# Attention scores and running maxima as pairs of 64-row matmuls, eight pairs to a group, in a one-core decoder layer

## What is computed

```python
q, k, v = (proj(Wq), proj(Wk), proj(Wv))             # H, DK = 16, 64
scores = jnp.einsum('bhqd,bhkd->bhqk', q, k)         # S = 2048
scores = scores + rel_bias[buckets(S)].transpose(2, 0, 1)[None]
attn = jax.nn.softmax(scores, axis=-1)
ctx = jnp.einsum('bhqk,bhkd->bhqd', attn, v)
```

## Time and profile before

| | |
|---|---|
| time, median of 3 runs | 3967.45 us (3962.96 to 3972.64) |
| span of the profiled execution | 3970.6 us |
| PE busy | 3864.0 us, 97% |
| DVE / ACT / POOL busy | 2459.6 / 2034.9 / 2685.8 us |
| granted clock of PE, mean | 0.989 |
| DMA, mean | 89 GB/s |

### The profile page before, as it was taken

One profiled execution on the slowest core, in us unless ns is written; L12 is line 12 of the kernel. 1 busy time (PEld: TensorE's weight loads), 2 busy tenths in 40 slices (PEclk: granted clock), 3 DMA queues, 4 the chain that ended last, 5 costly groups with the idle time before them and its releaser, 6 DMA issues. The chain is left out here.

```text
span 3970.6 us, 59813 instructions
## 1 busy us (share of the span) xinstructions
PE 3864.0 (97%) x18973; PEld 2189.4 (55%) x18973; DVE 2459.6 (62%) x3356; ACT 2034.9 (51%) x3452; POOL 2685.8 (68%) x1402
## 2 busy tenths in 40 slices
PE   8999999999999999999999999999997999997899
PEld 7754444444444444444444444444446888885477
DVE  3456666666666666666666666666634777775632
ACT  3335555555555555555555555555543555553232
POOL 1128888888888888888888888888893434430010
PEclk9989999999999999999999999999998999998999
DMA  7642222322222352222332222332312333335710
GB/s 222 168 104 57 62 60 62 94 74 62 62 59 62 93 161 60 64 60 59 87 85 60 64 59 60 88 83 59 100 34 83 107 101 103 106 104 174 278 45 22
DMA packets 395504, 352.29 MB, mean 89 GB/s; under 512 B 193947, under 2 KB 268187, under 8 KB 394008
## 3 DMA queue, kind: packets, MB, share of 16 engines
q1 hardware_dynamic: 326200, 321.84, 28.2%
q10 hardware_dynamic: 67168, 20.98, 2.2%
q0 software_dynamic: 1920, 6.29, 0.5%
HBM read 142.64 MB, written 89.70 MB: 59 GB/s over the span
## 5 line engine op out<-in xcount | busy, mean ns | idle before, releaser
L328 POOL TENSOR_TENSOR acc<-acc,probs 128x1024 f32<-128x1024 f32 x894 | 2127.2, 2379 | 263.5 <-ACT probs L798 138.7
L928 DVE TENSOR_REDUCE maxes<-ps 128x1 f32<-128x1024 f32 x1024 | 1251.2, 1222 | 700.9 <-PE ps L579 696.4
L801 ACT ACTIVATE probs<-ps,far_bias 128x1024 f32<-128x1024 f32 (+7 forms) x1280 | 1022.0, 820 | 1018.5 <-DVE near_s L945 561.2
L614 PE MATMUL ps<-probs,v_head 128*64 128x512 f32 x4096 | 992.2, 605 | 2.1 <-ACT ctx_out L784 2.0
L579 PE MATMUL ps<-stacks 64*128 64x512 f32 x2048 | 751.1, 447 | 16.4 <-issue 7.4
L594 PE MATMUL ps<-stacks 64*128 64x512 f32 x1792 | 662.1, 449 | 0.0
L593 PE MATMUL ps<-stacks 128*128 128x512 f32 x2048 | 619.2, 419 | 0.3 <-ACT probs L798 0.3
L594 PEld LDWEIGHTS ps<-stacks 64*128 64x128 f32 x1792 | 276.9, 185 | 501.0 <-issue 328.4
L614 PEld LDWEIGHTS ps<-probs,v_head 128*64 128x64 f32 x4096 | 248.6, 136 | 483.6 <-issue 481.4
L593 PEld LDWEIGHTS ps<-stacks 128*128 128x128 f32 x2048 | 351.3, 189 | 216.4 <-issue 164.0
L945 DVE TENSOR_TENSOR near_s<-ps,near_bias 128x384 f32<-128x384 f32 (+2 forms) x576 | 284.7, 494 | 268.9 <-PE ps L594 246.1
(11 more groups left out here) (281 smaller groups left out, 4751.7 us busy)
## 6 DMA issues: line engine op xcount, KB each, us to landing
stacks<-c_k SPq DMA_DIRECT2D x128, 256.0 KB, 2.5
stacks<-c_q SPq DMA_DIRECT2D x128, 256.0 KB, 2.6
stacks<-c_d SPq DMA_DIRECT2D x256, 128.0 KB, 2.7
scr_v<-probs ACTq DMA_DIRECT2D x32, 512.0 KB, 4.0
stacks<-c_q SPq DMA_DIRECT2D x128, 128.0 KB, 2.7
v_head<-scr_v SPq DMA_DIRECT2D x32, 512.0 KB, 3.6
scr_ctx<-ctx_out SPq DMA_DIRECT2D x128, 128.0 KB, 2.3
both_ctx<-scr_ctx SPq DMA_DIRECT2D x32, 512.0 KB, 4.0
```

The lines of the kernel that those rows point to most:

```text
L328: pool.tensor_tensor(acc[:, qb, :], acc[:, qb, :], pr, ALU.add).then_inc(s["summed"], 1)
L614: mm = pe.matmul(ps[64 * half:64 * half + 64, PV, :], v_head[:, side, kt, :], probs[:, st % PT_RING, half * 512:(half + 1) * 512], start=k ...
L801: ins = act.activation(probs[:, st % PT_RING, a:z], sc[:, a:z], ACT.Exp, bias=bias)
L928: dve.tensor_reduce(maxes[:, qt, pair:pair + 1], ps[:, bank:bank + 2, :], AX.XY, ALU.max).then_inc(s["max_done"], 1)
```

## The change

All score and maximum matmuls become 64-row matmuls in pairs that share the array: lanes 0 and 1 (rows 0 to 63 and 64 to 127) hold the same keys, and each owns half of the queries. A step is three pairs (key difference high by query high, by query low, and key difference low by query high), plus a guard pair in the first two steps of a queries half. A pair of maxima gives 512 keys against two tiles of queries. In a group PE does one pair of maxima, six pairs of scores, one pair of maxima in one run, then the projection, then the values. `stacks` is laid out anew, so `fill` issues 32 DMAs of 64 rows instead of 21; the guard row is loaded by two DMAs instead of one. On ACT and DVE both steps of a group come before the work of the projection that stood between them.

```diff
-FILLS_MAX, FILLS_SCORE = 16 * 2 * BLOCKS, 16 * (3 * BLOCKS + 1)
+FILLS_MAX, FILLS_SCORE, FILLS_GUARD = 16 * 3 * BLOCKS, 16 * 5 * BLOCKS, 32
...
 guard():
-                sp.dma_start(stacks[0:1, side, QB, half * QW:(half + 1) * QW]...).then_inc(s["neg_in"], 16)
+                for part in range(2):
+                    sp.dma_start(guard_q[guard_row(part, half), :]...).then_inc(s["neg_in"], 16)
...
 fill():
-                    sp.dma_start(stacks[:, side, KX, cols].bitcast(F32), c_k[:, cols]).then_inc(s["fill_max"], 16)
-                    sp.dma_start(stacks[:, side, QA, cols].bitcast(F32), c_q[:, cols]).then_inc(s["fill_max"], 16)
+                    for half in range(2):
+                        sp.dma_start(stacks[lane(half), side, KH, cols].bitcast(F32), c_k[0:64, cols]).then_inc(s["fill_max"], 16)
+                    sp.dma_start(stacks[lane(tb % 2), side, QS, q_high].bitcast(F32), c_q[0:64, cols]).then_inc(s["fill_max"], 16)
...
                     for half in range(2):
-                        sp.dma_start(stacks[64 * half:64 * half + 64, side, KA, cols].bitcast(F32), c_d[0:64, own]).then_inc(s["fill_score"], 16)
-                    sp.dma_start(stacks[64:128, side, QB, cols].bitcast(F32), c_q[0:64, cols]).then_inc(s["fill_score"], 16)
-                sp.dma_start(first_keys[64:128, side, :].bitcast(F32), c_k[64:128, 0:LOOKBACK]).then_inc(s["fill_score"], 16)
+                        sp.dma_start(stacks[lane(half), side, KD, cols].bitcast(F32), c_d[0:64, own]).then_inc(s["fill_score"], 16)
+                        sp.dma_start(stacks[lane(half), side, KL, cols].bitcast(F32), c_k[64:128, cols]).then_inc(s["fill_score"], 16)
+                    sp.dma_start(stacks[lane(tb % 2), side, QS, q_low].bitcast(F32), c_q[64:128, cols]).then_inc(s["fill_score"], 16)
...
 PE, new functions in place of max_half, score and row_tiles:
+            def largest(n, side, g, pair):
...
+                for half in range(2):
+                    mm = pe.matmul(ps[:, max_bank(n, pair) + half, :], stacks[lane(half), mside, QS, q], stacks[lane(half), mside, KH, keys],
+                                   start=True, stop=True)
+                mm.then_inc(s["maxed"], 1)
+            def scores(n, side, st):
...
+                past(pe, s["exped"], n * STEPS + st - 1)
+                if kt < 2:
+                    if kt == 0:
+                        pe.wait_ge(s["neg_in"], FILLS_GUARD * (2 * n + qb + 1))
+                    for half in range(2):
+                        pe.matmul(ps[:, bank + half, :], guard_keys[lane(half), qb, :], guard_q[lane(half), :], start=True, stop=True)
+                for of_keys, of_queries in ((KD, q_high), (KD, q_low), (KL, q_high)):
+                    for half in range(2):
+                        mm = pe.matmul(ps[:, bank + half, :], stacks[lane(half), side, of_keys, keys], stacks[lane(half), side, QS, of_queries],
+                                       start=False, stop=True, skip_group_check=True)
+                mm.then_inc(s["scored"], 1)
...
 PE, head():
+                    if has_max(n, g):
+                        largest(n, side, g, 0)
                     if own:
...
-                    row_tiles(n, side, g, 0, own, own and not start)
...
+                        scores(n, side, 2 * g)
+                        scores(n, side, 2 * g + 1)
+                    if has_max(n, g):
+                        largest(n, side, g, 1)
                     if prep and g in PROJ_GROUPS:
                         project(n + 2, *PROJ_GROUPS[g])
...
-                    row_tiles(n, side, g, 1, own, own and not start)
...
 ACT, head():
                         exp(n, k, side, 2 * g)
+                        exp(n, k, side, 2 * g + 1)
                     if prep and g in EVAC_GROUPS:
                         take_out(n + 2, EVAC_GROUPS[g])
...
-                    if own:
-                        exp(n, k, side, 2 * g + 1)
...
 DVE, head():
                         near(n, k, side, 2 * g)
+                        near(n, k, side, 2 * g + 1)
                     if stepped:
                         step(*stepped)
-                    if own:
-                        near(n, k, side, 2 * g + 1)
```

More of the change, by code:

```diff
@@ L212, in proj_bank, with max_bank @@
             return (PB, SC, SC + 1, MX + 1)[tb] if isinstance(m, int) and m == 0 else PB
[L214 removed]
+        def max_bank(n, pair):
             early = isinstance(n, int) and n < 0
[L217 removed]
+            return (MX, SC)[pair] if early else MX
         def value_bank(v):
@@ L565, in project @@
                     mm.then_inc(s["proj"], 1)
-            def max_half(n, side, g, pair, i):
-                late, qt = max_tile(g)
+            def largest(n, side, g, pair):
+                late, turn = max_turn(g)
                 m, mside = (n + 1, 1 - side) if late else (n, side)
[L571 to L575, removed]
-                    else:
-                        past(pe, s["max_done"], NT * 2 * m + 2 * qt + pair)
-                kc = 2 * pair + i
-                mm = pe.matmul(ps[:, max_bank(n, qt, pair) + i, :], stacks[0:64, mside, QA, qt * P:(qt + 1) * P],
-                               stacks[0:64, mside, KX, kc * 512:(kc + 1) * 512], start=True, stop=True)
-                if i == 1:
-                    mm.then_inc(s["maxed"], 1)
@@ L584, in score @@
-            def score(side, st, half, kind):
+                qt, first_chunk = max_tiles(turn)
+                if late and g == FIRST_MAX and pair == 0:
+                    pe.wait_ge(s["fill_max"], FILLS_MAX * (m + 1))
+                if isinstance(n, int) and n < 0:
+                    past(pe, s["max_done"], 2 * turn + pair - 1)
+                else:
+                    past(pe, s["max_done"], GROUPS * 2 * m + 2 * turn + pair)
+                q = slice((qt // 8 * 4 + qt % 8) * P, (qt // 8 * 4 + qt % 8 + 1) * P)
@@ L589, in score @@
-                out = ps[:, SC + 2 * (st % 2) + half, :]
-                if kind == "first":
-                    return pe.matmul(out, first_keys[:, side, keys], stacks[:, side, QB, q], start=True, stop=True)
-                if kind == "high":
-                    return pe.matmul(out, stacks[:, side, KA, keys], stacks[:, side, QA, q], start=False, stop=True, skip_group_check=True)
-                return pe.matmul(out, stacks[64:128, side, KX, keys], stacks[64:128, side, QB, q], start=False, stop=True, skip_group_check=True)
@@ L596, in row_tiles @@
-            def row_tiles(n, side, g, which, own, base):
-                for i in range(2):
-                    if base:
-                        mm = score(side, 2 * g + which, i, "low")
-                    if has_max(n, g):
-                        max_half(n, side, g, which, i)
-                if base and which == 1:
-                    mm.then_inc(s["scored"], 1)
+                q_high = slice(qb * 512, (qb + 1) * 512)
+                q_low = slice(QL + qb * 512, QL + (qb + 1) * 512)
```

75 lines of the change are left out of this document (35 added, 40 removed).

## The result

| | median, us | lowest to highest | ratio to the kernel before, 95% interval |
|---|---|---|---|
| kernel before, 4 runs | 3969.37 | 3962.96 to 3972.64 | |
| changed kernel, 4 runs | 4146.57 | 4143.06 to 4149.49 | 1.0443 [1.0428, 1.0457] |

A forecast was written before the change was run, and what follows sets the result against it. PE bounds the heads, POOL next. Groups 80.6 + fill 4.8 + DVE's queue 4.9 + clock 1.0 = 91.3 us a head, 6.4 more than now, over some 28 heads: about 4140 us, range 4030 to 4200.

The forecast's parts named there:

- The groups by themselves: PE's groups in a head: fewer mode changes bring it from 84.9 to 80.6 us, if nothing else waits.
- rival 4: Long runs of pairs: each pair costs 0.33 us instead of keeping 0.235, about 4240 us; chance 0.07.
- The fill: At g = 4: 32 DMAs at 0.64 us issue each end late and hold the second maxima, 4.8 us a head.
- Rival 2: The fill at g = 4 stays hidden because it ends by bytes, about 3980 us; chance 0.08.
- landing keeps pace: In the fill: DMAs land as fast as SP issues them, 0.64 us of issue each.
- DVE's queue: At the ends of blocks (g = 0, 4, 8, 12): steps behind exponentials and near additions delay maxima, 4.9 us a head.
- The clock: Behind the wait at g = 4: PE's granted clock drops to its lower level once a head, 1.0 us lost.
- Rival 1: At g = 4 the wait is there but the clock stays up, 4112 us; chance 0.20.
- The sum: All terms over a head: 91.3 us, 6.4 more than now, giving about 4140 us in total.
- Rival 3: In the heads only the saved mode changes count: 80.6 us a head, about 3840 us; chance 0.08.

The follow-up runs named there:

- e9_early: Changed kernel with a split wait for the fill, the old ACT and DVE order, and the guard store right behind the fill in SP's queue: 3886.47 us.
- e10_28: Changed kernel with high and low keys exchanged in lane 1, so the fill takes 28 DMAs instead of 32 for the same bytes: 4072.53 us.
- e5_old_32: Kernel before with only its fill cut into 32 DMAs of the same bytes instead of 21: 4199.84 us.
- e1_few: Changed kernel with the 20 DMAs of the fill's second part merged into 6 larger ones of 64 rows: 4159.57 us.
- e4_zeros: Changed kernel with 24 extra 64-row matmuls adding zeros in g = 4 of each head, while PE would wait: 4113.18 us.

## Why the prediction was right, and where its terms were not

*The groups by themselves, 80.6 us.* Right within 1.2 us: with its waits taken away the head is 81.8 us (e9_early). Part of that lies in the head before: the same lengths give 84.2 us for it, not the measured 84.9, so they promised 3.7 us saved and not 4.3. Measured are 3.1. The run of eight pairs holds its pace (six pairs, L621, in 1.55 us with a matmul's 0.39 at the end: 0.23 from pair to pair), and the second maxima come 1.82 us after the first, as worked out from DVE's reduction; rival 4, that long runs of pairs are slower, falls. Under the loss of 177 us lay a gain of some 80 us.

*The fill, 4.8 us.* Right mechanism, sized too small: PE's wait at g = 4 is 6.0 us (median; ACT's copy waits 168.5 us over 28 heads, as much), and not the 6.5 that I took for it in the expectations. The issue price of 0.64 holds (0.59 to 0.66 by e10_28), and the copy came 26.2 us into the head (a median over the heads) instead of 25.3. The other part is that g = 4 began 20.9 us into the head, not at 21.8. Rival 2, by which the fill would have stayed hidden, gave 3980 us; e5_old_32 and e10_28 speak against it. The rule of the Trainium skill that was set beside it (page "DMA: Bandwidth & Descriptors", section "Issuing engines are not separate DMA queues": initiating is usually small relative to the DMA itself) is no help at these sizes. A DMA costs SP 0.64 us here, and 128 KB at the rate of e1_few's backlog 0.55. (The fill before moves 3648 KB, not the 3712 written there, since its last DMA has 64 KB; by bytes it would have grown by 12%, 1.6 us.) The prediction's "landing keeps pace" held, but only just, as e1_few showed: the transfers of 64 rows are almost as long as their issues.

*DVE's queue, 4.9 us.* This step was too large. I added losses of 1.7 at g = 0/1 and 12/13 and 1.3 behind g = 4. By the table, the order costs 0.75 at g = 0 and 13 together, and returning it gives 12 us in all. The step also took the terms as separate. They are not: a loss ahead of g = 4 only shortens the wait for a fill whose end does not depend on it. That is why this term's error and the fill's cancelled: up to the end of the wait at g = 4 the head is as long as the fill makes it, however the time before is spent. With the fill out of the way the order is worth 1.5 us a head. It is not all of DVE's delay: PE's idle time in front of g = 1 and 13, ended by DVE's maxima, is 0.64 and 0.85 us a head in the changed kernel and still 0.20 and 0.50 in e9_early, with the old order (means of 26 heads).

*The clock, 1.0 us.* Right in place, 1.2 by e4_zeros. Rival 1, a clock that stays up, is out.

*The sum.* 6.4 us a head was forecast; the head went from 84.9 to 90.9. The forecast's total rests on two errors of opposite sign, fill and clock too small (5.8 against the 8.0 by which g = 4 exceeds its 4.11) and a queue too large (4.9 against 2.0, which is what the other groups exceed the prediction's lengths by: 0.6 at g = 0, 0.5 each at 12 and 13, 0.4 at 1 and 5 together). That 4140 came within 7 us of 4147 is therefore in part luck; the mechanism at g = 4 is not. The range had a slip as well: with the queue's own lower bound of 2 its low end takes off 2.9 a head, not 2.5, and comes to some 3995 instead of 4010. *Rival 3*, 3840 us if nothing else waited, is what the repairs come near to: 3886.

## What to carry to other kernels

When a change splits full-height copies into half-height ones, count DMAs in the queue and follow the last one to whoever waits for all of them; here 11 more issues of 0.64 us outweighed a better matmul schedule. A wait should name only what is overwritten: a semaphore for the first block turned 177 us of loss into a gain. Losses ahead of a fixed point don't add to it, and when that point goes, look for what was hidden behind it: here it was DVE's wait for the sums, whose DMAs stand behind the fill in SP's queue.

## What was not expected of the hardware

Larger DMAs of 64 rows did not help: behind two of them SP's issues stretch from 0.60 to some 2.2 us, and landing goes from 2.4 to 8 us. Adding 24 matmuls of zeros a head made the kernel 33 us faster, because PE's granted clock stayed up. In 27 of the changed kernel's 28 fills one to three issues take 0.9 to 2.4 us instead of 0.60 (at 1827.72 above); why was not tried.
